# Graph network, last stage: a copy of 128 x 256 features moved from VectorE to ScalarE

## The chip, the cores and the metric

The kernel runs on one core of a Trainium2 chip. The metric is the time of the whole program on the device in microseconds (us), as the median of several runs. A core has engines that run their own queues side by side: TensorE (PE in the profile, its weight loads PEld), VectorE (DVE), ScalarE (ACT), GpSimd (POOL) and SyncE (SP), which here issues most of the plain transfers. They meet through semaphores.

## The reference

Two graph layers over 6250 nodes of 256 features and 200,000 edges, each followed by a residual sum and a normalization:

```python
x = _layernorm(x + _L0_gnn_ref(x, src, dst, edge_weight, W))
x = _layernorm(x + _L1_gnn_ref(x, src, dst, ...))
```

The second layer sums messages of edges into `context` and `kron_feat` for each node. What the last stage of the kernel computes of it is this, where `node_feats` is the `x` that the first line gave:

```python
gi = context @ W_ih.T + b_ih
gh = node_feats @ W_hh.T + b_hh
i_r, i_z, i_n = jnp.split(gi, 3, axis=1)
h_r, h_z, h_n = jnp.split(gh, 3, axis=1)
r = jax.nn.sigmoid(i_r + h_r)
z = jax.nn.sigmoid(i_z + h_z)
n = jnp.tanh(i_n + r * h_n)
h = (1.0 - z) * n + z * node_feats
gru_out = layer_norm(jax.nn.relu(h), g_ln, beta_ln)
cat = jnp.concatenate([gru_out, kron_feat], axis=1)
return jax.nn.relu(layer_norm(cat @ Wc + bc, gc, betac))
```

`node_feats` is needed twice: in `h`, and at the very end in the residual sum `x + L1(x)`.

## The kernel before

Everything is float32. The stages run one after the other: the edges are sorted into tiles, the first layer's messages are gathered and summed, the node tables are made, the second layer's edges are worked through, and a last stage goes once over the nodes. The change lies in this last stage alone.

The last stage cuts the nodes into 49 tiles of 128. Each engine has its own written-out order, and `last_loop` runs it: tile 0 by itself, then a hardware loop whose body holds two tiles (buffers q = 0 and 1), then the rest. Let t be the tile.

- SyncE loads the tile's rows of x into `xf[q]` (L663, semaphore `f_x`). The load of tile t+2 goes into the same buffer and waits for `f_cat` of tile t. SyncE also stores the result (L667).
- TensorE, in `last_products`: transposes of the context and of x for tile t+1 (L1824, semaphore `f_t`), the final product of tile t-1 (L2185, L2187, bank `ps[4 + 3q]`), the gate products of tile t+1 (L2163, L2166, L2168, L2171, `f_gate`), then transposes of tile t's features (`f_ct`). L2185 waits for VectorE's copy L1792 of the turned features (`f_cts`).
- ScalarE, in `functions`: copy of the turned inputs of tile t+1 out of PSUM (`turned`, L1106), tanh of tile t (L1122), the square root of tile t's variance (L1116), two more square roots for tile t-1, and the sigmoids of tile t+1 (L1112). Sigmoid and tanh on the one side and the square root on the other need different tables, so there are two table loads in a tile, at L1116 and L1112.
- VectorE, in `last_stage`: the copy L1792 of tile t-1's turned features, then `features(t)`: r times h_n and the sum (L1759, L1760, semaphore `f_n0`), the copy of `xf[q]` into `xr[q]` (L1762), the node's kron sums with their bias into the right half of `cat` (L1766), after the tanh the blend with z (L1770 to L1773), the norm (L1462, L1464, L1468, L1469) and its scale and shift (L1775, L1776). Then the context of tile t+2 (L1748 to L1752) and `result(t-1)`: a norm of the final product, scale, shift, the residual sum with `xr[1 - q]` (L1784), and the last norm.

`xr` exists because the result of tile t is made a tile later, when the buffer `xf[q]` is being filled anew. `step` is VectorE's chain: it lets an instruction raise the engine's own semaphore and makes the queue wait for it before what follows. `PER2` is the number of such steps in a tile.

Of the kernel before, what the change touches and what calls it, by code (L numbers as in the profile page):

```python
# [49 lines left out]
ACT = mybir.ActivationFunctionType  # L50
# [37 lines left out]
def is_zero(i):  # L88

    return isinstance(i, int) and i == 0  # L90
# [7 lines left out]
def gnn_program(nc, io, V, E, EP):  # L98
# [30 lines left out]
    with ExitStack() as ctx:  # L129
# [3 lines left out]
        def sem(name):  # L133
            return ctx.enter_context(nc.semaphore(name))
# [25 lines left out]
        def cutter(arena):  # L160
# [106 lines left out]
        xf, xr = [[c(D) for _ in range(2)] for _ in range(2)]  # L267
# [108 lines left out]
        f_w, f_wp, f_ws, f_x, f_pre, f_t, f_ts, f_gate, f_sig, f_n0, f_tanh = (sem("f_" + n) for n in (  # L376
            "weights_loaded", "weights_turned", "weights_turned_sbuf", "x1_loaded", "context", "turned",
            "turned_sbuf", "gates", "sigmoid", "candidate", "tanh"))
# [7 lines left out]
        def nth(i, head=0):  # L386
            return i + 1 + head
# [3 lines left out]
        def last_loop(engine, body, before=None, after=None):  # L391

            pairs = (NT - 3) // 2
            body(0, 0)
            if before:
                before()
            with engine.Fori(0, pairs) as it:
                if before:  # L400
                    before(it)
                for q in range(2):
                    body(it * 2 + (1 + q), 1 - q)
            if after:
                after(pairs)
            for t in range(1 + 2 * pairs, NT):
                body(t, t % 2)

        def is_tile(t):

            return not isinstance(t, int) or 0 <= t < NT

        def tiles_of(engine, tiles, g, n):

            _, v = nc.values_load_multi_w_load_instructions(
                tiles[0:1, bass.ds(g, n)], engines=[engine], min_val=0, max_val=NT - 1,
                skip_runtime_bounds_check_because="the map is clamped to the last tile")
            return v

        def first_rows(firsts, g, n):  # L420

            _, v = nc.values_load_multi_w_load_instructions(
                firsts[0:1, bass.ds(g, n)], engines=[ENG.SP], min_val=0, max_val=E,
                skip_runtime_bounds_check_because="the rows are clamped to the edges' number")
            return v
# [54 lines left out]
        def _(sp):  # L480
# [145 lines left out]
            def load_m(it):  # L626

                for u in range(UN):
                    _, row_m = nc.values_load_multi_w_load_instructions(
                        m_row[0:1, bass.ds(it * (UN * SG) + u * SG, SG)], engines=[ENG.SP], min_val=0, max_val=KM * (NBK - 1),  # L630
                        skip_runtime_bounds_check_because="the buckets are clamped to their number")
                    for s in range(ST):
                        past(sp, e_h, it * (UN * SG) + (u * SG + (s + 1) * G - SG))
                        sp.sem_inc(e_gate, 1)
                        for i in range(s * G, (s + 1) * G):
                            sp.dma_start(m_ring[0:KM, i, :], m_rows[bass.ds(row_m[i], KM), :]).then_inc(e_mld[s], 16)
                    if not is_zero(it) or u == 3:
                        store_sums(it * UN + (u - 3), u - 3)
# [232 lines left out]
        def _(act):  # L871
            step = Chain(act, act_steps)
# [231 lines left out]
            def turned(t):  # L1104
                act.wait_ge(f_t, nth(t))
                nc.scalar.activation(tr4, ps[:, 0, :], ACT.Copy).then_inc(f_ts, 1)  # L1106

            def sigmoids(t, q):
                act.wait_ge(f_gate, nth(t))
                if not is_zero(t):  # L1110
                    act.wait_ge(f_cat, nth(t - 1))
                nc.scalar.activation(rz, ps[:, 1 + 4 * q, :], ACT.Sigmoid).then_inc(f_sig, 1)  # L1112

            def deviation(var, std, i):
                act.wait_ge(var, nth(i))
                nc.scalar.activation(st[:, 8:9], st[:, 7:8], ACT.Sqrt, bias=eps_c[:, :]).then_inc(std, 1)  # L1116

            def functions(t, q):
                if is_tile(t + 1):
                    turned(t + 1)  # L1120
                act.wait_ge(f_n0, nth(t))
                nc.scalar.activation(wb, wa, ACT.Tanh).then_inc(f_tanh, 1)  # L1122
                deviation(f_var, f_std, t)
                if is_tile(t - 1):
                    for i in range(2):
                        deviation(f_var2, f_std2, (t - 1) * 2 + i)
                if is_tile(t + 1):
                    sigmoids(t + 1, 1 - q)

            turned(0)  # L1130
            sigmoids(0, 0)
            last_loop(act, functions)
            for i in range(2):
                deviation(f_var2, f_std2, (NT - 1) * 2 + i)
# [3 lines left out]
        def _(dve):  # L1138
            step = Chain(dve, dve_steps)
# [305 lines left out]
            with dve.Fori(0, NG // 4) as it:  # L1445
                step.loop(held, it, 4)
                nt = tiles_of(ENG.DVE, tile_of, it * 4, 4)
                for u in range(4):
                    g, q = it * 4 + u, u % 2
# [286 lines left out]
            def last_norm(out, src, var, std, i):  # L1736
                norm_stats(src, var)
                return normalize(out, src, std, nth(i))

            def sums_at(t, lo):  # L1740
                return hrow[:, 2 * MSG * t + lo:2 * MSG * t + lo + MSG] if isinstance(t, int) else \
                    hrow[:, bass.ds(t * (2 * MSG) + lo, MSG)]

            def context_of(t, q):

                att = sums_at(t, MSG)
                dve.wait_ge(f_h[q], t * 8 + (16 - 8 * q))
                step(ts(st[:, 10:11], att[:, D:MSG], 1e-30, None, ALU.max))  # L1748
                step(nc.vector.reciprocal(st[:, 11:12], st[:, 10:11]))
                if not is_zero(t):  # L1750
                    dve.wait_ge(f_t, nth(t - 1))
                ts(ctx_f, att[:, 0:D], st[:, 11:12], 0.0, ALU.mult, ALU.max).then_inc(f_pre, 1)  # L1752

            def features(t, q):

                ksum, gates_n = sums_at(t, 0), ps[:, 2 + 4 * q, :]

                dve.wait_ge(f_sig, nth(t))
                step(tt(wa, rz[:, 0:D], gates_n[:, D:2 * D], ALU.mult))  # L1759
                tt(wa, wa, gates_n[:, 0:D], ALU.add).then_inc(f_n0, 1)  # L1760
                dve.wait_ge(f_x, 16 * (t + 1))
                step(nc.vector.tensor_copy(xr[q], xf[q]))  # L1762

                if not is_zero(t):
                    dve.wait_ge(f_ct, nth(t - 1))
                step(stt(out=cat[:, D:2 * D], in0=betak_b[:, :], scalar=ksum[:, D:MSG], in1=ksum[:, 0:D],  # L1766
                         op0=ALU.mult, op1=ALU.add))

                dve.wait_ge(f_tanh, nth(t))
                step(tt(wa, xf[q], wb, ALU.subtract))  # L1770
                step(tt(wa, wa, rz[:, D:2 * D], ALU.mult))
                step(tt(wa, wa, wb, ALU.add))
                step(ts(wa, wa, 0.0, None, ALU.max))  # L1773
                step(last_norm(wb, wa, f_var, f_std, t))
                step(tt(wb, wb, gln_b, ALU.mult))  # L1775
                tt(cat[:, 0:D], wb, bln_b, ALU.add).then_inc(f_cat, 1)  # L1776
# [12 lines left out]
            def turned_features(t):  # L1789
                dve.wait_ge(f_ct, nth(t))  # L1790
                past(dve, f_lin, t)
                nc.vector.tensor_copy(cat_t, ps[:, 3, :]).then_inc(f_cts, 1)  # L1792

            def last_stage(t, q):
                if is_tile(t - 1):
                    turned_features(t - 1)
                features(t, q)
                if is_tile(t + 2):
                    context_of(t + 2, q)
                if is_tile(t - 1):  # L1800
                    result(t - 1, 1 - q)

            PER2 = 18
            start = [0]

            def enter(it=None):
                if it is None:
                    start[0] = step.done
                else:
                    step.loop(start[0], it, 2 * PER2)  # L1810

            context_of(0, 0)
            context_of(1, 1)
            last_loop(dve, last_stage, enter, lambda n: step.loop_ended(start[0], n, 2 * PER2))
            turned_features(NT - 1)
# [411 lines left out]
```

## Time and profile before

| | us |
|---|---|
| median of 3 runs | 8837.32 |
| the runs | 8832.91 to 8851.87 |
| the profiled execution | 8825.73 |
| its span, first to last instruction | 8824.2 |

The profile is that of one execution. Its rows of instructions give a start, a duration, the engine, the line of the kernel and what is written from what. A row's square bracket is the time that the engine stood idle before it, and what ended that. The granted clock is TensorE's, as a share of 2.4 GHz.

### The profile page before, as it was taken

Reading aid. Unit: us, or ns where it says so; the run is one execution under the profiler, and the core shown is the slowest. Engines: PE = TensorE matmul, PEld = TensorE weight load, DVE = VectorE, ACT = ScalarE, POOL = GpSimd, SP = SyncE. Lnnn points to the kernel's source line nnn. Section 1 sums busy time; section 2 is a strip of 40 time slices with the busy share of each in tenths; the row PEclk is TensorE's granted clock in tenths of the full one; section 3 lists DMA queues with packets and bytes.
Section 4 is the critical chain, followed back from the end, with each engine's and each line's share of the span. In section 5 each row is a group of like instructions: output and inputs, shape, how many; then the busy total and the mean of one; then the engine's idle time right before and its main releaser. Section 6 shows DMA issues by size and latency. Waiting matters only on the chain.

```text
span 8824.2 us, 170071 instructions
## 1 busy us (share of the span) xinstructions
PE 6448.5 (73%) x32727; PEld 4092.5 (46%) x32728; DVE 5665.5 (64%) x16285; ACT 4050.2 (46%) x11127; POOL 4402.1 (50%) x4339
## 2 busy tenths in 40 slices
PE   5254666666666999877777777777777777777998
PEld 4123444444444777633344444444444444444444
DVE  8784444444444666655477777777777777776777
ACT  7243444444443000033266665656666566655333
POOL 0005777777776000000077777777777777775100
PEclk9686778888888999966699999999999999999988
DMA  0113333333323888755577777777777777776100
GB/s 13 1 36 102 103 104 103 104 103 103 102 101 113 262 262 263 235 225 223 222 211 210 208 207 200 206 200 208 207 204 206 205 208 201 205 205 177 55 19 18
DMA packets 973553, 1399.03 MB, mean 159 GB/s; under 512 B 378858, under 2 KB 744924, under 8 KB 960328
## 3 DMA queue, kind: packets, MB, share of 16 engines
q1 hardware_dynamic: 761663, 797.51, 30.1%
q0 software_dynamic: 208448, 596.38, 24.0%
q14 instruction: 418, 3.42, 0.1%
q10 hardware_dynamic: 3012, 1.51, 0.1%
q8 instruction: 12, 0.20, 0.0%
HBM read 986.32 MB, written 415.51 MB: 159 GB/s over the span
## 4 chain that ended last, share of the span: by engine, by line
PE 32%; DVE 17%; issue 17%; DMA 14%; SPq 8%; ACT 8%; POOL 2%; DVEq 2%; ACTq 1%; POOLq 0%
DMA arena_n<-rec_dram 9%; SPq L559 7%; PE ps L2029 6%; PE ps L1927 5%; PE ps L1824 4%; ACT junk L1026 4%; PE ps L2047 3%; PE ps L2038 3%; DMA arena_e<-msg_dram 2%; PE ps L1942 2%; DVE arena_r L1328 2%; DVE arena_e L1605 2%; DVE arena_e L1665 2%; POOL msg_dram L823 2%; ACT L1047 1%
## 5 line engine op out<-in xcount | busy, mean ns | idle before, releaser
L844 POOL DMA_INDIRECT arena_n<-tab_dram,idxs x2624 | 2747.2, 1047 | 2505.2 <-DVE idxs L1580 1574.2
L2029 PE MATMUL ps<-arena_n 126*128 126x257 f32 x5234 | 1713.1, 423 | 661.7 <-DVE arena_e L1605 642.3
L823 POOL DMA_INDIRECT msg_dram<-arena_e,idxq x1616 | 1582.7, 979 | 510.9 <-issue 455.1
L2029 PEld LDWEIGHTS ps<-arena_n 126*128 126x128 f32 x5234 | 855.0, 196 | 1241.3 <-DVE arena_e L1605 1088.0
L1916 PE MATMUL ps<-arena_n,arena_r 128*128 x3232 | 1019.4, 469 | 354.8 <-ACT arena_r L935 354.8
L1605 DVE COPY arena_e<-ps 128x257 f32<-128x257 f32 x1962 | 815.8, 421 | 644.9 <-ACT junk L1026 631.3
L1026 ACT ACTIVATE junk<-ps 128x256 f32<-128x256 f32 x2617 | 985.0, 381 | 305.7 <-PE ps L2029 244.4
L1665 DVE SCALAR_TENSOR_TENSOR arena_e<-arena_e,rstd,nbetak_b 128x256 f32<-128x256 f32 x2608 | 1086.9, 479 | 31.5 <-DVE rstd L1671 30.1
L940 ACT ACTIVATE arena_e<-ps,recq 128x256 f32<-128x256 f32 x1616 | 730.7, 474 | 594.2 <-PE ps L1916 587.6
L1916 PEld LDWEIGHTS ps<-arena_n,arena_r 128*128 128x128 f32 x3232 | 710.1, 231 | 585.6 <-issue 474.5
L1016 ACT ACTIVATE arena_n<-ps 126x512 f32<-126x512 f32 x655 | 391.0, 597 | 1130.6 <-PE ps L1824 977.9
L1927 PE MATMUL ps<-arena_e,oh 128*128 128x256 f32 x3520 | 817.2, 387 | 84.7 <-DVE oh L1357 83.5
L1142 DVE TENSOR_SCALAR recq<-arena_n 128x16 f32 (+1 forms) x404 | 101.6, 252 | 1039.1 <-DMA arena_n<-rec_dram 542.0
L1927 PEld LDWEIGHTS ps<-arena_e,oh 128*128 128x128 f32 x3520 | 642.2, 190 | 260.1 <-issue 155.8
L1824 PE MATMUL ps<-ident,arena_n 128*126 128x128 f32 (+1 forms) x3109 | 537.4, 284 | 192.5 <-ACT arena_n L1049 124.0
L1824 PE MATMUL ps<-ident,oh 128*128 128x128 f32 x1616 | 327.9, 339 | 419.4 <-issue 361.8
L1824 PEld LDWEIGHTS ps<-ident,arena_n 128*126 128x126 f32 (+1 forms) x3109 | 410.1, 145 | 413.4 <-issue 344.4
L1026 ACT ACTIVATION_READ_ACCUMULATOR junk<-ps 128x1 f32 x2617 | 535.1, 204 | 0.0
L1824 PEld LDWEIGHTS ps<-ident,oh 128*128 128x128 f32 x1616 | 249.1, 177 | 533.1 <-issue 423.6
L935 ACT ACTIVATE arena_r<-ps 128x512 f32<-128x512 f32 x404 | 241.2, 597 | 517.0 <-PE ps L1824 500.6
L2038 PE MATMUL ps<-arena_e,oh 128*32 128x257 f32 x5216 | 473.5, 409 | 0.0
L1594 DVE TENSOR_TENSOR arena_n<-arena_n,oh 128x504 f32<-128x504 f32 x656 | 444.5, 678 | 28.7 <-DMA arena_n<-tab_dram,idxs 21.7
(342 smaller groups left out, 8972.1 us busy)
## 6 DMA issues: line engine op xcount, KB each, us to landing
arena_n<-m_dram SPq DMA_DIRECT2D x2624, 126.5 KB
arena_e<-msg_dram SPq DMA_DIRECT2D x441, 514.0 KB, 4.5
m_dram<-arena_e SPq DMA_DIRECT2D x49, 1413.5 KB, 4.9
m_dram<-arena_e SPq DMA_DIRECT2D x49, 1285.0 KB, 4.5
arena_n<-tab_dram,idxs POOLq DMA_INDIRECT x2624
hist_dram<-arena_r SPq DMA_DIRECT2D x163, 253.0 KB
arena_n<-rec_dram SPq DMA_DIRECT2D x1616, 2.0 KB
msg_dram<-arena_e,idxq POOLq DMA_INDIRECT x1616
```

The lines of the kernel that those rows point to most:

```text
L559: sp.dma_start(at(rec_all, it * G + j, 4, 4), rec_dram[bass.ds(start[j], P), :]).then_inc(s_recs, 16)
L823: nc.gpsimd.indirect_dma_start(out=msg_dram, in_=msgs[:, u, j, :], in_offset=None, out_offset=bass.IndirectOffsetOnAxis(ap=idxq[:, u, j:j ...
L844: nc.gpsimd.indirect_dma_start(out=feat[:, u, i, :], out_offset=None, in_=tab_dram, in_offset=bass.IndirectOffsetOnAxis(ap=idxs[:, u, i:i ...
L940: nc.scalar.activation(msgs[:, u, j, 0:D], ps[:, 2 + j, 0:D], ACT.Copy, scale=recq[:, u, 4 * j + 2:4 * j + 3]).then_inc(m_msg, 1)
L1026: nc.scalar.activation(junk[:, i % 2, 0:D], ps[:, bank_of(i), 1:HC], ACT.Square, scale=1.0 / 16, accum_out=var[:, u % 2, i:i + 1]).then_in ...
L1605: nc.vector.tensor_copy(hgb[:, u % 2, i, 0:HC], ps[:, bank_of(i), 0:HC]).then_inc(e_hg, 1)
L1665: stt(out=h, in0=h, scalar=rstd[:, u % 2, i:i + 1], in1=nbetak_b[:, :], op0=ALU.mult, op1=ALU.max).then_inc(e_clip, 1)
L1824: return nc.tensor.transpose(out, src, ident[:, :])
L1916: mm(ps[:, 2 + j, 0:D], oh_t[:, q, j * P:(j + 1) * P], at(x_all, nt[u * G + j], D, MSG), start=True, stop=True).then_inc(m_x, 1)
L1927: ins = mm(ps[:, q, 0:D], oh[:, q, j * P:(j + 1) * P], msgs[:, u, j, 0:D], start=(j == 0), stop=(j == G - 1))
L2029: mm(ps[:, bank_of(i), 0:HC], prods_t[0:KM, s % 2, j * P:(j + 1) * P], m_ring[0:KM, i, :], start=True, stop=True).then_inc(e_h, 1)
L2038: mm(ps[32 * j:32 * (j + 1), 4, 0:MSG], oh[:, u, 32 * i:32 * (i + 1)], hgb[:, u % 2, i, 1:1 + MSG], start=(s == 0), stop=(s == ST - 1)).th ...
```

## The change

The copy of `xf[q]` into `xr[q]` leaves VectorE's `features` and stands in ScalarE's `functions`, between the copy of the turned inputs (L1106) and the tanh (L1122), with a wait for the load ahead of it. VectorE keeps its own wait for the load. The number of steps that VectorE's loop counts per tile falls by one.

```diff
@@ -1118,6 +1118,8 @@
             def functions(t, q):
                 if is_tile(t + 1):
                     turned(t + 1)
+                act.wait_ge(f_x, 16 * (t + 1))
+                nc.scalar.activation(xr[q], xf[q], ACT.Copy)
                 act.wait_ge(f_n0, nth(t))
                 nc.scalar.activation(wb, wa, ACT.Tanh).then_inc(f_tanh, 1)
                 deviation(f_var, f_std, t)
@@ -1759,7 +1761,6 @@
                 step(tt(wa, rz[:, 0:D], gates_n[:, D:2 * D], ALU.mult))
                 tt(wa, wa, gates_n[:, 0:D], ALU.add).then_inc(f_n0, 1)
                 dve.wait_ge(f_x, 16 * (t + 1))
-                step(nc.vector.tensor_copy(xr[q], xf[q]))
 
                 if not is_zero(t):
                     dve.wait_ge(f_ct, nth(t - 1))
@@ -1800,7 +1801,7 @@
                 if is_tile(t - 1):
                     result(t - 1, 1 - q)
 
-            PER2 = 18
+            PER2 = 17
             start = [0]
```

## Rows read from the trace of the kernel before

**Rows 1.** The page, busy time and share of the span of each engine.
```profile
PE 6448.5 (73%) x32727; PEld 4092.5 (46%) x32728; DVE 5665.5 (64%) x16285; ACT 4050.2 (46%) x11127; POOL 4402.1 (50%) x4339
```

**Rows 2.** Busy time by stretch: stretch, us, each engine, granted clock, DMA share, GB/s.
```profile
8150.00:8798.00 648.00, 596.59 (x1810) 316.28 (x1810) 478.21 (x1378) 238.30 (x382) 34.15 (x36) 0.90 0.11 34
...
8282.00:8297.00 15.00, 14.45 (x38) 7.24 (x38) 10.31 (x31) 6.07 (x11) 0.00 (x0) 0.77 0.08 26
```

**Rows 3.** Waits, 8150 to 8824: who waited for whom, us in total, times, longest.
```profile
PE ps L2185 <- DVE arena_e L1792: 55.8, 48, 4.7
...
DVE arena_e L1792 <- PE ps L1824: 42.0, 18, 4.4
...
DVE arena_e L1759 <- ACT arena_e L1112: 26.3, 32, 10.1
```

**Rows 4.** The copy's line: count, ns min/median/max, first and last start.
```profile
L1762 DVE COPY arena_e<-arena_e x49: 284/285/333, 8150.6 to 8799.4; 128x256 f32<-128x256 f32 x49
```

**Rows 5.** Timeline, one tile: start us, us, engine, line, what.
```profile
8256.85 0.42 DVE L1759 TENSOR_TENSOR arena_e<-arena_e,ps 128x256 f32<-128x256 f32 x1 [0.70 <-ACT arena_e L1112]
...
8267.61 0.29 ACT L1116 ACTIVATE st<-st,eps_c 128x1 f32<-128x1 f32 x1 [3.00 <-DVE st L1464]
...
8267.93 1.28 ACT L1112 ACT_TABLE_LOAD   x1
...
8269.22 0.60 ACT L1112 ACTIVATE arena_e<-ps 128x512 f32<-128x512 f32 x1
...
8269.71 0.59 ACT L1106 ACTIVATE arena_e<-ps 128x512 f32<-128x512 f32 x1
8269.85 0.42 DVE L1759 TENSOR_TENSOR arena_e<-arena_e,ps 128x256 f32<-128x256 f32 x1 [0.46 <-ACT arena_e L1112]
...
8270.30 0.42 DVE L1760 TENSOR_TENSOR arena_e<-arena_e,ps 128x256 f32<-128x256 f32 x1
8270.64 0.28 DVE L1762 COPY arena_e<-arena_e 128x256 f32<-128x256 f32 x1
8270.76 0.42 ACT L1122 ACTIVATE arena_e<-arena_e 128x256 f32<-128x256 f32 x1 [0.45 <-DVE arena_e L1760]
8271.12 0.48 DVE L1766 SCALAR_TENSOR_TENSOR arena_e<-betak_b,arena_n 128x256 f32<-128x256 f32 x1 [0.19 <-DVE arena_e L1762]
...
8271.64 0.42 DVE L1770 TENSOR_TENSOR arena_e<-arena_e 128x256 f32<-128x256 f32 x1
```

**Rows 6.** The chain that ended last, in that tile; DVEq is VectorE's queue.
```profile
8270.97 0.10 DVEq L1766
8271.07 0.05 issue
```

**Rows 7.** Timeline of the stage, single rows of L1792, ScalarE and L2185.
```profile
8158.54 0.69 DVE L1792 COPY arena_e<-ps 128x512 f32<-128x512 f32 x1 [2.13 <-PE ps L1824]
...
8184.57 0.69 DVE L1792 COPY arena_e<-ps 128x512 f32<-128x512 f32 x1
...
8200.94 0.69 DVE L1792 COPY arena_e<-ps 128x512 f32<-128x512 f32 x1 [3.40 <-PE ps L1824]
...
8281.47 0.68 DVE L1792 COPY arena_e<-ps 128x512 f32<-128x512 f32 x1
...
8296.26 0.69 DVE L1792 COPY arena_e<-ps 128x512 f32<-128x512 f32 x1 [1.71 <-PE ps L1824]
8296.69 0.60 ACT L1106 ACTIVATE arena_e<-ps 128x512 f32<-128x512 f32 x1 [0.28 <-PE ps L1824]
...
8297.76 0.42 ACT L1122 ACTIVATE arena_e<-arena_e 128x256 f32<-128x256 f32 x1 [0.47 <-DVE arena_e L1760]
...
8309.21 0.69 PE L2185 MATMUL ps<-arena_e,ones 1*128 1x256 f32 x2 [1.05 <-DVE arena_e L1792]
...
8401.68 0.69 PE L2185 MATMUL ps<-arena_e,ones 1*128 1x256 f32 x2 [1.30 <-DVE arena_e L1792]
...
8798.00 0.69 DVE L1792 COPY arena_e<-ps 128x512 f32<-128x512 f32 x1 [4.36 <-PE ps L1824]
```

## Prediction

> **What bounds the kernel now.** The page comes first: TensorE is busy 73% of the span, but that is a mean over stages [rows 1], and the change touches only the last one, 49 tiles in the last 8% of the span. So I read the busy time by stretch next. From 8150 to 8798 us TensorE is busy 597 of 648 us, VectorE 478, ScalarE 238, at a mean granted clock of 0.90 [rows 2]. Two engines are close to full there, and ScalarE has room. The list of waits in the stage says how they share the bound [rows 3]: TensorE waits 55.8 us in 48 tiles for VectorE's copy of the turned features (L1792), VectorE waits 42.0 us in 18 tiles for TensorE's transposes before that same copy, and 26.3 us in 32 tiles for ScalarE's sigmoid (L1112). A tile is therefore bound in one of two ways, and the timeline tells which.
>
> A tile bound by VectorE and ScalarE: L1759 starts at 8256.85 and again at 8269.85, 13.00 us later [rows 5]. The way round is one chain, from L1759 through all of VectorE's work to the third square root (8267.61), then ScalarE's table load (8267.93, 1.28 us), the sigmoid (8269.22, 0.60 us), and the next L1759. Everything VectorE loses between L1759 and that square root lengthens the tile.
>
> A tile bound by TensorE: L1792 follows the one before by 14.79 us (8281.47 to 8296.26) after VectorE had waited 1.71 us for transposes [rows 7]. In that stretch the granted clock is 0.77 on average [rows 2], a mixture of 1.00 (2.4 GHz) and 0.50 (1.2 GHz); one long stretch at the lower level makes the tile from 8184.57 to 8200.94 last 16.37 us [rows 7]. What TensorE did just before: it had stood still, waiting for L1792. It stands there after every such tile for 1.29 or 1.30 us, as at 8401.68 [rows 7], because VectorE then starts late and needs its full round.
>
> Adding up: from the first L1792 (8158.54) to the last but one (8798.00) are 47 spacings in 639.5 us [rows 7]. At 13.00 each they would be 611.0; the other 28.5 us come from 17 tiles in which VectorE really lost time to TensorE (the 18 of [rows 3], less the first, which lies ahead of the count), 1.68 us each.
>
> **The change part by part.** *Removed from VectorE:* one copy of 128x256, 285 ns, 49 times [rows 4]. In the tile of [rows 5] the copy starts at 8270.64, at once behind L1760, and its successor L1766 starts at 8271.12. That is 0.48 us: 0.28 of copy, then a wait for its end, then 0.10 us of address arithmetic and 0.05 us of issue that could not start earlier [rows 6]. With the copy gone L1766 has no such wait, since it reads nothing that L1760 writes. It starts at 8270.64 if the arithmetic fits under L1760, and at 8270.79 if all 0.15 us come behind. It takes 0.48 to 0.50 and L1770 follows 0.03 later: 8271.16 to 8271.32.
>
> L1770 has a second condition, the tanh of L1122: 8270.76 plus 0.42 ends at 8271.18, so L1770 can't start before 8271.21. It started at 8271.64. The gain of a tile is thus 0.32 to 0.43 us, not the 0.48 that leaves the queue. I take 0.38, the middle, because other register work on this queue seems partly covered. The wait on the tile's loaded rows stays in VectorE's queue, so nothing is gained there, and behind it stands only L1766, whose data is long there.
>
> *Added to ScalarE:* a wait on the same load, and a copy of 128x256 from SBUF to SBUF, 49 times. Nothing on ScalarE in this stage has just that form. The nearest row is the tanh, same shape and memories: 0.42 us [rows 5]. From below: the sigmoid and L1106 start 0.49 apart for twice the elements, so a copy of half the size could hold the engine as little as 0.25; from above, the 0.60 us of a whole 512 wide activation. It stands between L1106 (start 8269.71, busy 0.59) and the tanh, where ScalarE idles from 8270.30 to 8270.76. Successive activations overlap a little (8269.22 and 8269.71), so the copy starts between 8270.20 and 8270.30. At 0.42 us it ends by 8270.72, ahead of the tanh. I cost it at nothing; the cover is the wait for L1760's sum. In the TensorE-bound kind L1106 starts at 8296.69 and the tanh at 8297.76 [rows 7], the same 1.07 us, so the cover is equal. At 0.60 us the copy would end at 8270.80 to 8270.90 and tanh would be 0.04 to 0.14 late: the gain of a tile drops from 0.38 to about 0.29 at worst. The copy and L1106 are both plain copies, and L1106 stands between sigmoid and tanh today without a table load, so I add none. The queue behind the new wait holds tanh and the square roots; the load was issued two tiles earlier, so the wait is over when reached.
>
> The Trainium skill speaks against the move: "ScalarE: Activation LUTs", section "Rules for kernel authors", puts cheap elementwise work on VectorE and budgets about 0.3 us an activation plus 0.83 ns an element. For 256 elements that is an estimate of 0.51 us; the tanh's row says 0.42. By the page the copy would end at 8270.71 to 8270.81, so tanh at most 0.05 late, and the gain would fall to between 0.33 and 0.38.
>
> *Moved:* no DMA. The load of tile t+2 still waits for L1776 of tile t, which comes 0.38 earlier; the result's store likewise.
>
> *Sum at unchanged clock.* The 0.38 counts in each tile but those where VectorE next waits for TensorE anyway: 49 less 17 is 32, and 32 x 0.38 = 12.2 us. The same in the other form: 47 x 12.62 = 593.1, plus 17 x (1.68 + 0.38) = 35.0, is 628.1 against 639.5: 11.4, and 0.4 each for what lies outside.
>
> *What TensorE's clock gives back.* A shorter VectorE tile also shortens TensorE's wait ahead of L2185. The timeline's 48 such waits show where the clock falls. Behind none of the 20 up to 1.05 us did it fall ([rows 7] has the longest of them and one of 1.30); of the 13 of 1.29 or 1.30 us it fell behind 9; of the 14 of 1.62 to 2.32 us behind 9; the last, 4.71, lies at the end. The wait of 1.29 is the one that follows a TensorE-bound tile, and it keeps the alternation of a long and a short tile going. It becomes about 0.91, which is in the harmless class; the 1.62 and 2.08 become 1.24 and 1.70, still in the dangerous one. So the alternation every second tile breaks, but falls go on elsewhere: I estimate 15 in place of 17. Then 593.1 + 15 x 2.06 = 624.0, a gain of 15.5, and with the ends 16 us.
>
> **The numbers.** The profiled execution took 8825.7 us with a span of 8824.2; the sum puts it at 8810. The median of the runs is 8837.3, 11.6 above the profiled one; the same subtraction gives 8821 us, 0.18% less. This is just inside what a measurement of this kernel can tell from no change: 0.2% is 17.7 us.
>
> **Rivals.**
> *The clock hardly falls any more.* If waits of 1.24 are harmless like those of 1.05, only the waits of 1.70 count, about every other VectorE-bound tile and not always. With 8 falls: 593.1 + 16.5 = 609.6, a gain of 30, 8807; with none 46, 8791. For it: no fall up to 1.05. Against it: 9 falls in 13 at 1.29, only 0.05 away. Chance 0.15.
>
> *Falls as often as now.* The clock falls 17 or 18 times: gain 11 to 12, 8826. [...] Chance 0.2, beside 0.47 for 13 to 16 falls (gain 13 to 20).
>
> *ScalarE becomes late.* The copy takes 0.6 us or more, or brings a table load of 1.28 us. With 0.6 us the gain is 32 x 0.29 = 9, 8828. With a table load tanh would be 1.1 us late, 32 x 0.7 = 22 us slower than before, 8860. Against: L1106 needs none. Chance 0.05 and 0.01.
>
> *Slower through the clock.* A tile of 12.62 us may fall into step with the clock's decisions so that every third wait is followed by a long fall (the tile of 8184.57 to 8200.94 was 16.37 us, 3.4 over 13, or 3.8 against 12.62). It passes the old time at (639.5 - 593.1) / 3.75 = 12 such falls, and the 0.2% at 17: 593.1 + 63.8 = 656.9, 8855. There were 5 such long ones before. For it: which waits are answered by a fall is not set by their length alone. Chance 0.05, two thirds of it beyond 0.2%.
>
> *The change does nothing:* L1766 waits for something else not seen. Then 8837. Chance 0.07.
>
> **From cases to chances.** Faster by over 0.2% (17.7 us) are the first rival, a good third of the likeliest case (13 falls and a gain of 0.43 a tile reach 21), and, since repeated runs of this kernel spread by 19 us (8832.9 to 8851.9), a tenth more from the other cases: 0.15 + 0.17 + 0.08 = 0.40. Slower: 0.05. Same: 0.55. The range leaves out the last of the clock's gains and the late ScalarE: 8804 to 8838. The likeliest case's own range is 8813 to 8828.
>
> **What would show it.** L1762 gone from VectorE; L1766 0.34 us behind L1760; L1770 at 1.33 to 1.47 us after L1759 (now 1.79); a VectorE-bound tile of 12.57 to 12.68; a new activation between L1106 and L1122 of 0.42 us, and L1122 still 0.04 behind L1760's end; no table load more than now; TensorE's wait ahead of L2185 at 0.9 where it was 1.29, and 13 to 16 waits of L1792 for TensorE in place of 18. The prediction is wrong if tanh comes late, if L1766 keeps its distance, or if those waits grow in number.

## The result, and the profile after

The changed kernel takes 8806.28 us (median of 8 runs, 8795.65 to 8826.52), the kernel before 8841.05 us (8 runs, 8832.05 to 8858.72). The ratio is 0.9963, 95% interval 0.9954 to 0.9973: 0.37% faster, some 35 us. The forecast was 8821 us, 0.18% faster, with a range of 8804 to 8838. The time lies in the range, 2 us above its lower end. The direction was right; the size was half of what came, and the likelier class ("within 0.2%", 0.55) was not the one that came true.

The profiled execution took 8800.76 us. The last stage begins later than in the profile of before, its first turned features are copied at 8171.47 against 8158.54 us [rows 7], so the stages ahead, which the change doesn't touch, were 12.9 us slower in this execution. Inside the last stage, from the first copy of turned features to the last but one, 47 spacings take 601.8 us in place of 639.5: 37.7 us less. Lines have moved by one or two: L1792 is L1793 now, L1759 is L1761, L2185 is L2186, and the new activation stands at L1122, the tanh at L1124.

Busy time of that stretch, the same columns as in [rows 2]:

```profile
8171.47:8773.26 601.79, 555.45 (x1786) 303.54 (x1786) 458.44 (x1313) 247.22 (x424) 30.03 (x31) 0.95 0.11 34
```

The mean granted clock has risen to 0.95; it was 0.90 [rows 2]. The waits of the stage, as in [rows 3]:

```profile
PE ps L2186 <- DVE arena_e L1793: 51.8, 49, 4.7
...
DVE arena_e L1761 <- ACT arena_e L1112: 30.7, 39, 10.3
...
DVE arena_e L1793 <- PE ps L1825: 18.4, 15, 4.0
```

VectorE waited 42.0 us for TensorE's transposes in 18 tiles and now waits 18.4 us in 15. The number hardly fell, the length more than halved. That is the main thing to see. (Of the waits for ScalarE's sigmoid, 26.3 us before and 30.7 now, 10.1 and 10.3 us are one single wait at the beginning of the stage, ahead of the 47 spacings.)

The timeline of one tile bound by VectorE, which answers to [rows 5]:

```profile
8402.61 0.60 ACT L1112 ACTIVATE arena_e<-ps 128x512 f32<-128x512 f32 x1
...
8403.10 0.59 ACT L1106 ACTIVATE arena_e<-ps 128x512 f32<-128x512 f32 x1
8403.24 0.42 DVE L1761 TENSOR_TENSOR arena_e<-arena_e,ps 128x256 f32<-128x256 f32 x1 [0.46 <-ACT arena_e L1112]
...
8403.58 0.42 ACT L1122 ACTIVATE arena_e<-arena_e 128x256 f32<-128x256 f32 x1
8403.69 0.42 DVE L1762 TENSOR_TENSOR arena_e<-arena_e,ps 128x256 f32<-128x256 f32 x1
8404.03 0.48 DVE L1767 SCALAR_TENSOR_TENSOR arena_e<-betak_b,arena_n 128x256 f32<-128x256 f32 x1
8404.15 0.42 ACT L1124 ACTIVATE arena_e<-arena_e 128x256 f32<-128x256 f32 x1
...
8404.66 0.43 DVE L1771 TENSOR_TENSOR arena_e<-arena_e 128x256 f32<-128x256 f32 x1 [0.16 <-ACT arena_e L1124]
...
8415.88 0.42 DVE L1761 TENSOR_TENSOR arena_e<-arena_e,ps 128x256 f32<-128x256 f32 x1 [0.70 <-ACT arena_e L1112]
```

ScalarE's copy lies between 8403.58 and 8404.00 and is done 0.15 us before the tanh, which starts 0.04 us behind the end of L1762's sum, as before. The kron sums (L1767) follow the sum at 0.34 us. The blend (L1771) starts 1.42 us after L1761, where it was 1.79, and now waits for the tanh. The tile takes 12.64 us, from 13.00.

The next rows show a tile in which the clock fell. First the timeline, then the busy time of three stretches (the same columns as in [rows 2]; 1.00 is 2.4 GHz, 0.50 is 1.2 GHz):

```profile
8275.73 0.69 DVE L1793 COPY arena_e<-ps 128x512 f32<-128x512 f32 x1
8276.88 0.42 DVE L1761 TENSOR_TENSOR arena_e<-arena_e,ps 128x256 f32<-128x256 f32 x1 [0.46 <-ACT arena_e L1112]
...
8288.86 0.69 DVE L1793 COPY arena_e<-ps 128x512 f32<-128x512 f32 x1 [0.64 <-PE ps L1825]
8289.52 0.42 DVE L1761 TENSOR_TENSOR arena_e<-arena_e,ps 128x256 f32<-128x256 f32 x1
```

```profile
8272.00:8276.00 4.00, 2.75 (x16) 2.26 (x16) 3.15 (x9) 1.34 (x2) 0.00 (x0) 1.00 0.00 0
8277.00:8279.00 2.00, 2.00 (x5) 1.39 (x5) 1.78 (x5) 1.83 (x4) 0.00 (x0) 0.50 0.01 4
8281.00:8289.00 8.00, 8.00 (x28) 4.08 (x26) 5.84 (x19) 2.01 (x5) 0.00 (x0) 1.00 0.05 16
```

The clock was low for about 4 us here, read in steps of half a microsecond. VectorE waited 0.64 us for TensorE, and yet L1761 comes 12.64 us after the last one, as in any other tile: that wait fell where VectorE would have waited for the sigmoid (0.46 us in the first row, no wait in the last). This fall cost nothing.

### The profile page after: what moved, and what is told of

Same layout as the page of the kernel before. It is cut to its first block, busy times and chain, and to the rows that moved or that the text cites. A ratio compares the mean times of both kernels' runs of the same rounds, so it can differ in the third digit from the quotient of the medians.

```text
span 8799.3 us, 170048 instructions
## 1 busy us (share of the span) xinstructions
PE 6433.1 (73%) x32727; PEld 4094.2 (47%) x32728; DVE 5644.4 (64%) x16236; ACT 4063.5 (46%) x11176; POOL 4394.5 (50%) x4339
## 3 DMA queue, kind: packets, MB, share of 16 engines
q10 hardware_dynamic: 3012, 1.51, 0.1%
## 4 chain that ended last, share of the span: by engine, by line
PE 31%; DVE 18%; issue 17%; DMA 14%; ACT 8%; SPq 8%; POOL 2%; DVEq 2%; ACTq 1%; POOLq 0%
DMA arena_n<-rec_dram 9%; SPq L559 7%; PE ps L2030 6%; PE ps L1928 5%; PE ps L1825 5%; ACT junk L1026 4%; PE ps L2048 3%; PE ps L2039 3%; DMA arena_e<-msg_dram 3%; PE ps L1943 2%; DVE arena_r L1330 2%; DVE arena_e L1607 2%; DVE arena_e L1667 2%; ACT L1047 1%; POOL msg_dram L823 1%
## 5 line engine op out<-in xcount | busy, mean ns | idle before, releaser
L1596 DVE TENSOR_TENSOR arena_n<-arena_n,oh 128x504 f32<-128x504 f32 x656 | 444.4, 677 | 28.5 <-DMA arena_n<-tab_dram,idxs 22.2
```

## The experiments

They ran on four chips (e1 to e4 on one, e5 to e8, e9 with after_again, e10 with e11), on each of which the kernel before takes 11.1 to 11.3 ms. The extra time lies ahead of the last stage, and the last stage itself is as long there as on the first chip: after_again, the changed kernel unchanged, takes 603.2 us against 601.8, and e2_both, whose tile is 13.00 us like that of the kernel before, 640.0 against 639.5. The kernel before itself was profiled on the first chip only. So the reading goes by that stage: the 47 spacings named above, from one profile each; the first of them still overlap the end of the loads, so "above" can come out a little under zero. "Above" is what they take more than 47 times the spacing of L1759 in a VectorE-bound tile (its median over the stage). "Falls" are falls of TensorE's clock in the stage, the long ones being those with more than 4 us at the lower clock, read in steps of half a microsecond (in after_again and e1_no_copy the last of the 15 lies 1.5 us behind the 47 spacings). Only the changed kernel has two profiles, and they differ by 1.4 us: differences of that size between single profiles say nothing.

| kernel | tile, us | 47 spacings, us | above | falls (long) | ratio to the kernel before |
|---|---|---|---|---|---|
| before | 13.00 | 639.5 | 28.5 | 18 (16) | 1 |
| e2_both | 13.00 | 640.0 | 29.0 | 19 (18) | 0.9996 [0.9986, 1.0006] |
| e11_one_product | 13.00 | 618.3 | 7.3 | 9 (4) | one run |
| e10_two_products | 13.00 | 610.0 | -1.0 | 0 | one run |
| e3_warm_before | 13.00 | 609.9 | -1.1 | 0 | 0.9979 [0.9969, 0.9990] |
| e7_pad_c | 12.92 | 623.4 | 16.1 | 12 (7) | one run |
| e6_pad_b | 12.84 | 606.8 | 3.3 | 12 (2) | one run |
| e8_dma_copy | 12.75 | 604.3 | 5.1 | 12 (2) | one run |
| e5_pad_a | 12.72 | 606.1 | 8.2 | 13 (3) | one run |
| after | 12.64 | 601.8 | 7.7 | 14 (3) | 0.9963 [0.9954, 0.9973] |
| after_again | 12.64 | 603.2 | 9.1 | 15 (3) | 0.9960 [0.9944, 0.9977] |
| e1_no_copy | 12.64 | 603.2 | 9.1 | 15 (3) | 0.9969 [0.9956, 0.9982] |
| e4_warm_after | 12.63 | 592.7 | -0.9 | 0 | 0.9959 [0.9947, 0.9972] |
| e9_context_act | 12.38 | 582.0 | 0.1 | 0 | 0.9943 [0.9928, 0.9958] |

### No copy at all (e1_no_copy)

```diff
-                act.wait_ge(f_x, 16 * (t + 1))
-                nc.scalar.activation(xr[q], xf[q], ACT.Copy)
...
-                step(stt(out=yb, in0=ya, scalar=0.0, in1=xr[q], op0=ALU.max, op1=ALU.add))
+                step(stt(out=yb, in0=ya, scalar=0.0, in1=gc_b, op0=ALU.max, op1=ALU.add))
```

> Leaves out the copy altogether: neither engine makes it, and the last sum adds a constant tile instead of the node's rows, so the residual is not computed. Theory A (ScalarE's copy is fully covered by its wait for L1762's sum): the same time as the changed kernel, 8806 within 8 us, a tile bound by VectorE of 12.6 us. Rival B (the copy delays tanh, or the square root's table load behind it): 2 us or more faster per 0.05 us a tile, 8796 if tanh comes 0.2 us earlier, with L1771 closer to L1761 than 1.42 us.

The stage takes 603.2 us, the tile 12.64 us, and the blend starts 1.43 us after the first product, as with the copy. ScalarE's copy is free to within what one profile shows; theory A holds, the rival falls.

### Both engines copy (e2_both)

```diff
                 dve.wait_ge(f_x, 16 * (t + 1))
+                step(nc.vector.tensor_copy(junk[:, 0, 0:D], xf[q]))
...
-            PER2 = 17
+            PER2 = 18
```

> ScalarE copies as in the changed kernel, and VectorE makes its old copy too, into an unused buffer, with its wait. Theory A (only what VectorE loses or gains counts): the time of the kernel before, 8841 within 8 us, a VectorE-bound tile of 13.0 us and 17 or so waits of L1793 for TensorE that are long. Rival B (the added activation by itself disturbs ScalarE): slower than before by more than 8 us. Rival C (something else in the new order of the queues made the gain): clearly faster than 8830.

640.0 us, a tile of 13.00 us and 18 long falls: the stage of the kernel before, to half a microsecond, and a ratio that holds 1. The whole gain, with what the clock gives back, comes from VectorE's copy being gone.

### TensorE's wait filled, kernel before (e3_warm_before)

```diff
                 if is_tile(t - 1):
+                    for c in range(3):
+                        mm(ps[:, 7 - 3 * q, D:2 * D], wih_t[:, 0:P], whh_t[:, 0:D], start=True, stop=True)
                     final_products(t - 1, 1 - q)
```

> The kernel before, and TensorE fills part of its wait ahead of the final product with three 128x128x256 products that nothing reads, 0.7 us. Theory C (the lower clock costs 28 us in the stage before, and half the gain of the change is that this cost shrank): no or few falls of the clock in the stage, 47 spacings near 611 in place of 639 us, 8841 - 25 = 8816. Rival D (the clock's falls are not what costs; TensorE's own work is): no gain or slower, 8841 to 8860, since TensorE has more to do.

The clock doesn't fall once in the stage. Busy time of the 47 spacings, the same columns:

```profile
10609.23:11219.15 609.92, 585.51 (x2072) 336.93 (x2071) 472.40 (x1361) 231.63 (x376) 30.16 (x31) 1.00 0.11 34
```

609.9 us, 29.6 less than the kernel before, although TensorE has more to do. Theory C holds. One thing I had wrong: each product is two instructions of the array, so three of them fill not 0.7 but 1.5 us, as the timeline of one tile shows:

```profile
10802.34 1.04 PE L1824 MATMUL ps<-ident,arena_e 128*128 128x128 f32 x8
10803.22 1.46 PE L2195 MATMUL ps<-arena_r 128*128 128x256 f32 x6
10805.01 0.69 PE L2185 MATMUL ps<-arena_e,ones 1*128 1x256 f32 x2 [0.33 <-DVE arena_e L1792]
```

### The same in the changed kernel (e4_warm_after)

The same three lines in the changed kernel.

> The changed kernel with the same three products. Theory C: only 7.7 us of the 601.8 in its 47 spacings lie above 47 x 12.64, so at most 7 us are to be had, 8800; the difference between this kernel and the one before with the products is then VectorE's part alone, 47 x 0.36 = 17 us. Rival D: 8806 or slower, by as much as e3 is slower than before. If the two differ by 35 us as the kernels without products do, the clock has no part in the gain.

592.7 us, with the granted clock at 1.00 throughout:

```profile
10616.06:11208.71 592.65, 584.26 (x2072) 337.08 (x2071) 457.96 (x1314) 245.89 (x423) 29.16 (x30) 1.00 0.11 34
```

This splits the gain. Without any fall the change is worth 609.9 - 592.7 = 17.3 us. With the falls it is 37.7. So 20.4 us of the 37.7 are what the lower clock costs less than before: 29.6 (639.5 - 609.9) before, 9.1 (601.8 - 592.7) after. The expectation for this run had put the second at 7 at most.

### The copy as a second load (e8_dma_copy)

```diff
+            def keep_x1(t, q):
+                sp.dma_start(xr[q], rows(x1_dram, t)).then_inc(f_xr[q], 16)
...
+            keep_x1(0, 0)
+            keep_x1(1, 1)
...
                     store(t - 1)
+                    if is_tile(t + 1):
+                        keep_x1(t + 1, 1 - q)
...
-                act.wait_ge(f_x, 16 * (t + 1))
-                nc.scalar.activation(xr[q], xf[q], ACT.Copy)
...
                 step(tt(ya, ya, bc_b, ALU.add))
+                dve.wait_ge(f_xr[q], t * 8 + (16 - 8 * q))
```

> Neither engine copies: SyncE loads the node's rows a second time, straight into the buffer that the last sum reads, once the result that read it is done. It computes everything. Theory A (ScalarE's copy is free): the stage is as long as in the changed kernel, 602 us in 47 spacings, a VectorE-bound tile of 12.64. Rival B (ScalarE's copy holds up something after all): shorter than 595. Rival E (one more load and one more wait of VectorE's queue are seen): longer than 606.

604.3 us, but the tile is 12.75 us long, 0.11 more than with ScalarE's copy, which was not expected. The trace shows where: the last sum (L1792 there) starts 0.57 us behind the instruction before it, 0.46 in the changed kernel, and all starts of VectorE's tile ahead of it are the same to 0.01 us. The one thing added there is the wait for the load. The stage was within 3 us of the changed kernel's, since the falls cost 5.1 in place of 7.7; 604.3 lies between what theory A (602) and rival E (over 606) said, and the tile of 12.75 speaks for E. By the tile, ScalarE is the better place.

### A longer chain on VectorE, in three doses (e5_pad_a, e6_pad_b, e7_pad_c)

```diff
                 features(t, q)
+                nc.vector.tensor_copy(junk[:, 0, 0:256], betak_b[:, 0:256])
+                nc.vector.tensor_copy(junk[:, 1, 0:32], betak_b[:, 0:32])
```

This is e7_pad_c; e6_pad_b has the first of the two lines alone, e5_pad_a has it with 16 columns.

> The changed kernel, and VectorE makes one more copy of 128x16 into an unused buffer in each tile, about 0.07 us of its chain. The tile bound by VectorE becomes 12.71 us. Theory L (what TensorE's clock costs is a constant of some 8 us): 47 spacings of 597.4 + 8 = 605 us. Theory S (what the clock costs hangs on the tile's length, in steps): anywhere from 600 to 622.

> The same with one more copy of 128x256, 0.20 us of the chain; the tile becomes 12.84 us. Theory L: 603.5 + 8 = 611 us in 47 spacings. Theory S: 603.5 and 8 to 25 more.

> The same with two more copies, of 128x256 and 128x32, 0.28 us of the chain; the tile becomes 12.92 us, still 0.08 shorter than in the kernel before. Theory L: 607.2 + 8 = 615 us. Theory S: the long stretches at the lower clock are back, 630 to 645 us, as much as or more than the 639.5 of the kernel before with its longer tile.

The tiles came out at 12.72, 12.84 and 12.92 us as meant. Above the sum lie 8.2, 3.3 and 16.1 us. The step from 12.72 to 12.84 costs less than 1 us in 47 tiles, where the sum says 5.6, and the step from 12.84 to 12.92 costs 16.6 where the sum says 3.8. Each of the three has one profile, so the first step stands only as small, but 16.6 us is far beyond the 1.4 by which two profiles of one kernel differ. Theory L falls. Theory S holds in kind only: for e6_pad_b it said 8 to 25 above the sum and 3.3 came, for e7_pad_c 630 to 645 us and 623.4 came. Its falls are no more than those of e6_pad_b, 12 and 12, but 7 are long in place of 2.

### Less filling (e10_two_products, e11_one_product)

The lines of e3_warm_before in the kernel before, with two products and with one.

> The kernel before, its tile bound by VectorE still 13.00 us, and two unread products (0.5 us) in TensorE's wait ahead of the final product. Its waits of 1.29, 1.62 and 2.08 become about 0.8, 1.15 and 1.6, near those of the changed kernel. Theory W (the length of TensorE's wait sets what the clock costs): 8 us above 611, or 619, as in the changed kernel. Theory P (the tile's length sets it, whatever the wait): about 28 above 611, 639 or, since TensorE now has more to do in each tile, more.

> The same with one unread product, 0.25 us; the waits become about 1.05, 1.4 and 1.85. Theory W: between, 616 to 632 us in 47 spacings, near the kernel with a tile of 12.84 to 12.92 us (3 to 16 above its sum). Theory P: 639 or more.

Two products leave waits of 0.76 and 1.22 us ahead of the final product, in turn, and no fall comes in the 47 spacings: 610.0 us. One product leaves mostly 1.19 and 1.65 us and 9 falls, 8 of them behind waits of 1.65 us or more and one behind 1.40: 618.3 us. Each of them fills twice what I had written, so the waits are shorter than expected, and the 619 that theory W named for two products came with one. Theory P falls at once: the same tile of 13.00 us costs 28.5, 7.3 or nothing above its sum, according to how long TensorE stands.

### A version that beats both (e9_context_act), and the changed kernel beside it

```diff
-                ts(ctx_f, att[:, 0:D], st[:, 11:12], 0.0, ALU.mult, ALU.max).then_inc(f_pre, 1)
...
+                nc.scalar.activation(ctx_f, att, ACT.Relu, scale=st[:, 11:12]).then_inc(f_pre, 1)
```

The first line leaves VectorE's `context_of`, the second stands on ScalarE behind the first square root of the tile, with a wait for the reciprocal; the three products of e3_warm_before are in too.

> Meant to beat both: the changed kernel with the three products that fill TensorE's wait, and the context's scaling with its clip (128x256) made by ScalarE with Relu and a scale per row, where it waits for the second variance. It computes everything. The chain of VectorE loses 0.27 us a tile (start to start of L1754 and what follows), so 12.63 becomes 12.36, and 47 spacings 592.7 - 12.7 = 580 us. Rival: the activation comes later than VectorE's did, and TensorE's transposes of the inputs with it; or Relu brings a table load of 1.28 us beside the square roots: then over 640 us.

> The changed kernel once more, unchanged, on the chip of the run beside it. Every theory: the same stage as in its first profile, 602 us in 47 spacings within 5, and 0.4% less than the kernel before in whatever time that has on this chip.

e9_context_act: 0.9943 [0.9928, 0.9958] of the kernel before, against 0.9960 [0.9944, 0.9977] for the changed kernel on the same chip; the stage is 582.0 against 603.2 us. The intervals of the two ratios meet, the stages don't. The timeline (rows of VectorE, then of ScalarE) shows what binds it now:

```profile
10603.47 0.69 DVE L1803 COPY arena_e<-ps 128x512 f32<-128x512 f32 x1 [0.95 <-PE ps L1835]
```

```profile
10610.18 0.51 ACT L1124 ACTIVATE arena_e<-arena_n,st 128x256 f32 x1 [1.96 <-DVE st L1764]
10610.67 0.29 ACT L1117 ACTIVATE st<-st,eps_c 128x1 f32<-128x1 f32 x1
```

The activation fits in ScalarE's idle time and brings no table load. VectorE waits 0.95 us for TensorE in the tile shown, and it waits in all 47: with 1.5 us of filling TensorE has become the bound, at the full clock, with a tile of 12.38 us. VectorE's own chain got shorter than I expected: the instruction that gives the third variance starts 9.66 us after the tile's first product in place of 10.18, 0.52 us earlier where I had written 0.27, and the wait for TensorE takes up the rest. Fewer products would leave room for it; that was not run.

## Why the prediction was half right

**The cost on VectorE** was right. Predicted were 0.32 to 0.43 us a tile, 0.38 taken, a tile of 12.62 us and the blend at 1.33 to 1.47 us; measured are 0.36 to 0.37, 12.64 and 1.42. The tanh is what stops it at that, as said. With the clock kept high the change alone is worth 17.3 us in 47 spacings, 0.37 each.

**The cost on ScalarE** was right: 0.42 us, the duration taken from the tanh's row, hidden, no table load, the tanh not late. e1_no_copy shows it by itself. The estimate of 0.51 us from the Trainium skill ("ScalarE: Activation LUTs", "Rules for kernel authors") was too high for this copy (0.42 measured), and its case of a late tanh did not come. The cover that the prediction called the same 1.07 us in both kinds of tile is 1.05 in that of [rows 5].

**The number of falls** was right: 15 estimated in place of 17, 14 seen. The 15 had no sum behind it, so that it came so close is in part luck. The waits ahead of the final product behave by the classes that the prediction made. Behind none of the 29 up to 1.11 us did the clock fall; it fell behind 6 of the 8 of 1.24 to 1.26 us and behind 8 of the 11 of 1.37 to 1.81. The wait one round after a tile with a long fall, once 1.29 us, is now 0.70 to 1.11, and the alternation of a long and a short tile is gone, as said. One reading of before was too smooth: the wait one round after a TensorE-bound tile was 1.29 or 1.30 us in 13 of 16 cases, not in every one; the others are 1.05 (the one at 8309.21 in [rows 7]), 1.68 and 1.69.

**The price of a fall** is the step that failed: "593.1 + 15 x 2.06 = 624.0". The 2.06 was the mean price of the falls before (1.68) with the lost 0.38 added, and it assumed that the falls would be of the same kind. They are not. Before, 16 of 18 falls lasted 7 to 11 us; two consecutive tiles around one of 7 us take 27.24 us in place of 26.00. After, 11 of 14 last about 4 us, and these cost nothing, as the rows of 8276.88 and 8289.52 show for one; the next L1761 comes in time behind the others too. The 7.7 us above the sum are nearly all from the 3 long ones: 16.49 + 12.25, 14.78 + 11.85 and 16.48 + 11.85 us, each less 25.28, are 3.5, 1.4 and 3.1, together 7.9. The second of them:

```profile
8414.50 0.68 DVE L1793 COPY arena_e<-ps 128x512 f32<-128x512 f32 x1
...
8429.28 0.69 DVE L1793 COPY arena_e<-ps 128x512 f32<-128x512 f32 x1 [2.07 <-PE ps L1825]
```

The mean over 14 falls is 0.55, not 2.06, and 15 x 0.55 = 8.3 in the place of 30.9 would have given 8799 us for the median, too low by 7, within the spread of the runs.

The bound that I should have used was in the rows of before: a short fall (one at 8256.9, one at 8349.1) had delayed nothing there either. I took a mean over falls of unlike length, and let it stand for falls that would come at other places in the tile.

**Why the falls became short.** The place in the tile at which a fall begins goes with its length without an exception. In the ten profiles of the table that have falls there are 139; what one costs is read from the two spacings of VectorE's first product (L1759, L1761 after) that follow it. The 78 short ones begin 0.30 to 1.21 us after the final product's start and cost 0.02 us or less, but for two of 0.15 and 0.23 and a few at the end of the stage where it can't be read. The 31 of about 7 us begin 1.51 to 2.07 us after that start and cost 1.0 to 1.4 us. The 30 of 10.5 us begin within 0.26 us of it or 1.22 to 1.46 us after it and cost 2.8 to 3.5 us. The two kernels differ in where their falls begin: 11 of the 18 before at 1.85 to 2.07 us, 11 of the 14 after at 0.32 to 1.18. In these two profiles the two instructions of the bias product (L2163 before, L2164 after) take 1.22 and 1.06 us behind each of the 19 long falls, and the second takes 0.59 us, the time at the full clock, behind each of the 13 short ones. Whether the place causes the length was not tried: no run moved a fall within the tile and left the rest alone. Why the falls of the changed kernel begin earlier stays open too.

**What decides whether the clock falls** is shown in part. Filling the wait is enough to stop the falls (e3, e10 and e11 against the kernel before), and in no profile did the clock fall behind a wait of 1.22 us or less. Above that the wait's length alone doesn't decide: 9 of the 13 waits of 1.29 or 1.30 us were followed by a fall in the kernel before, 4 of the 19 of 1.34 to 1.47 us in e6_pad_b. The length of the tile moves the share of long falls unevenly (2 of 12 at 12.84 us, 7 of 12 at 12.92), which is worth up to 17 us for 0.08 us a tile.

**The rivals.** "The clock hardly falls any more" (0.15) named a gain of 30, which is about what came, but by another road: it is the length of the falls that went, not their number. "Falls as often as now" doesn't hold by count or by cost: 14 falls behind 49 waits, and 11 of them without a cost. The Trainium skill ("TensorE: Matmul & The Clock Gate", "HAM oscillation") tells of a kernel with thin tiles in which waits for DMA of about 3 to 5 us put the clock down in every round. This stage differs in both: its waits ahead of the final product are 2.3 us at most, and the clock falls behind some of them only, 18 of 48 before and 14 of 49 after. "ScalarE becomes late", "slower through the clock" and "the change does nothing" fell.

**The chances.** 0.40 for over 0.2% faster was low because the price of a fall was taken as known. The 20.4 us of the clock are larger than the 17.3 us of the instruction itself, and the whole difference between forecast and result sits in them.

## What to carry to other kernels

When two engines take turns as the bound, price a shorter chain twice: once as instructions times duration in the tiles where the chain binds, and once as what it does to TensorE's wait and so to its clock. In this stage the second term was the larger. Don't price a fall of the clock by a mean; see in the rows where in the tile it begins, how long the lower clock lasted and whether the next tile's first instruction was late at all. And where TensorE stands a little in each tile, first try to fill the wait with products that nothing reads: in the kernel before, three unread products a tile gained 29.6 us of the stage (a ratio of 0.9979 for the whole program) without touching any other engine.

## What the runs showed of the hardware that was not expected

Filling 1.0 us of TensorE's wait per tile (e10_two_products) removed all 18 falls of the clock from the 47 spacings and brought its mean granted clock from 0.90 to 1.00, at waits of 0.76 and 1.22 us that remain.

A longer tile can be as fast: 12.72 and 12.84 us a tile give 606.1 and 606.8 us for 47 spacings, and 12.92 gives 623.4, in one profile each.

Where a fall of the clock begins told how long it lasts, in all 139 falls of ten profiles: about 4 us when it began 0.30 to 1.21 us behind the final product's start, about 7 or 10.5 us elsewhere. The short ones cost next to nothing.

The experiments' chips ran the same kernel 25 to 28% slower as a whole (11.1 to 11.3 ms), with a mean granted clock of 0.78 in place of 0.88 over the span, and the last stage no slower at all. Where the rest goes was not looked into.
